# Attention and quantized FFN on one core: stacks loaded a batch earlier, FFN weights loaded and summed later

## What is computed

```python
# x: (8, 128, 256) float32, cond: (8, 256) mask; 16 heads of 8 channels
Q, K, V = proj(Wq), proj(Wk), proj(Wv)                    # per batch, from x
att = einsum('bhqd,bhkd->bhqk', Q, K) / sqrt(8) + b
att = att * m + (1 - m) * -1e30;  att = softmax(att)
y = einsum('bhqk,bhkd->bhqd', att, V)
# FFN over the channels; activations quantized per token to 8 bits,
# weights to -1, 0, 1 times the mean of their absolute values
h = silu(bit_linear(y, w_gate)) * bit_linear(y, w_up)
out = x + bit_linear(rms_norm(h) * ln_weight, w_down)     # (8, 128, 256)
```

## Time and profile before

| | |
|---|---|
| median of 3 runs | 175.95 us (175.43 to 178.37) |
| the profiled execution | 175.54 us, its span 173.7 us |
| busy in the span | PE 145.5, DVE 143.1, ACT 125.2, POOL 96.2 us |
| mean granted TensorE clock | 0.979 |

### The profile page before, as it was taken

The page is one execution under the profiler, slowest core; times in us unless marked ns, Lnnn a source line. Parts: engine busy times, 40 slices in busy tenths (PEclk is TensorE's granted clock), DMA queues, the critical chain, the costliest instruction groups (busy, mean ns, idle before and its releaser), DMA issues.

```text
span 173.7 us, 4104 instructions
## 1 busy us (share of the span) xinstructions
PE 145.5 (84%) x1395; PEld 68.1 (39%) x1402; DVE 143.1 (82%) x209; ACT 125.2 (72%) x253; POOL 96.2 (55%) x175
## 2 busy tenths in 40 slices
PE   7979894999989979969979999977699586887672
PEld 3664552433433423323323333322223264454561
DVE  6789895599999979869879898953678999999981
ACT  2041489699879869849869889878698928886651
POOL 5989507705808929829729629522040884677520
PEclk9999999699999999999999999999999969999999
DMA  4895988632232322622232320000000000010002
GB/s 118 287 167 131 303 304 284 167 91 55 61 93 57 74 75 57 203 65 57 68 80 59 92 52 3 3 6 5 0 0 4 0 2 0 30 34 30 32 30 91
DMA packets 20124, 14.19 MB, mean 82 GB/s; under 512 B 2160, under 2 KB 19080, under 8 KB 20104
## 3 DMA queue, kind: packets, MB, share of 16 engines
q1 hardware_dynamic: 17624, 10.91, 22.5%
q10 hardware_dynamic: 2480, 3.02, 6.2%
HBM read 6.17 MB, written 1.07 MB: 42 GB/s over the span
## 4 chain that ended last, share of the span: by engine, by line
PE 26%; SPq 17%; ACT 13%; DVE 12%; DMA 11%; issue 11%; ACTq 5%; POOL 2%; DVEq 0%; POOLq 0%
SPq L264 15%; PE y_ps L1000 7%; DMA k_st<-parts 6%; PE s_ps L962 5%; DMA w_f<-in_wuT 5%; ACT probs L523 4%; ACTq L264 4%; PE t_ps L980 4%; DVE hid L813 2%; DVE hw L822 2%; SPq L325 2%; ACT h_T L644 2%; PE y_ps L1041 1%; ACT hid_sq L627 1%; PE t_ps L1120 1%
## 5 line engine op out<-in xcount | busy, mean ns | idle before, releaser
L879 DVE TENSOR_REDUCE maxes<-s_ps 128x4 f32<-128x1024 f32 x64 | 76.1, 1217 | 11.4 <-PE s_ps L962 11.2
L523 ACT ACTIVATE probs<-t_ps 128x512 f32<-128x512 f32 x128 | 71.3, 593 | 15.9 <-PE t_ps L980 14.2
L962 PE MATMUL s_ps<-k_st,q_st 64*128 64x256 bf16 x256 | 44.9, 277 | 4.8 <-DMA k_st<-parts 4.5
L980 PE MATMUL t_ps<-q_st,k_st 64*128 64x256 bf16 x256 | 43.8, 277 | 4.7 <-ACT probs L523 3.1
L1000 PE MATMUL y_ps<-probs,v_pad 128*18 128x256 f32 x512 | 39.1, 388 | 0.0
L962 PEld LDWEIGHTS s_ps<-k_st,q_st 64*128 64x128 bf16 x256 | 15.8, 94 | 34.1 <-issue 12.8
L409 POOL TENSOR_SCALAR nm_parts<-maxes 128x16 bf16<-128x16 f32 x16 | 3.3, 208 | 33.6 <-DVE maxes L879 27.2
L478 POOL TENSOR_TENSOR hw<-hid,ln_bc 128x512 f32<-128x512 f32 x8 | 10.2, 1273 | 19.7 <-DVE hid L802 14.9
L1081 PE MATMUL s_ps<-w_q,ffn_x 128*128 128x512 bf16 x59 | 16.9, 387 | 3.3 <-DVE hid L813 1.5
L980 PEld LDWEIGHTS t_ps<-q_st,k_st 64*128 64x128 bf16 x256 | 14.7, 94 | 11.3 <-ACT probs L523 6.0
L1000 PEld LDWEIGHTS y_ps<-probs,v_pad 128*18 128x18 f32 x512 | 9.7, 96 | 13.6 <-issue 12.1
(11 more groups left out here) (106 smaller groups left out, 238.4 us busy)
## 6 DMA issues: line engine op xcount, KB each, us to landing
q_st<-parts SPq DMA_DIRECT2D x48, 64.0 KB
k_st<-parts SPq DMA_DIRECT2D x36, 64.0 KB
w_f<-in_wgT ACTq DMA_DIRECT2D x2, 512.0 KB, 5.4
w_f<-in_wuT ACTq DMA_DIRECT2D x2, 512.0 KB, 8.3
w_f<-in_wdT SPq DMA_DIRECT2D x2, 512.0 KB, 4.7
out<-o_sb SPq DMA_DIRECT2D x8, 128.0 KB, 1.7
k_st<-parts ACTq DMA_DIRECT2D x12, 64.0 KB
x_sb<-in_x SPq DMA_DIRECT2D x2, 256.0 KB, 4.0
```

The lines of the kernel that those rows point to most:

```text
L523: act.activation(probs[:, t % NP_RING].rearrange("p e t -> p (e t)"), src, ACT.Exp, scale=SCALE)\
L879: dve.tensor_reduce(dst[:, :, s, :], s_ps[:, c % 2], AX.X, ALU.max).then_inc(s_maxed, 1)
L962: mm = pe.matmul(s_ps[:, c % 2, i, e, :], q_st[b % RING][rows, hp, qt * P:qt * P + P], k_st[b % RING][rows, hp, :], start=True, stop=True)
L980: mm = pe.matmul(t_ps[:, u % T_BANKS, e, :], k_st[b % RING][rows, hp, kt * P:kt * P + P], q_st[b % RING][rows, hp, :], start=True, stop=True)
```

## The change

Four things change; what is computed, and how, does not.

1. SP loads the stack of batch n+3 in step n, where it loaded that of batch n+2. The order within a step is new: second maxima of batch n; rows, bias and all six high parts of batch n+3; first maxima of batch n+1; six low parts of batch n+3. Batch 1's stack is loaded ahead of the loop.
2. ACT issues weight pieces 0 to 3 in slot (-1, 7), a step's length later; SP issues 4 and 5 (and the last part of the mask) at the end of step 0 instead of step -1.
3. The sums are moved and dealt out anew: ACT takes q = 0, 2, 4, 5 in slots (0, 4), (0, 7), (1, 4), (2, 3); DVE takes q = 1, 3 in (0, 5), (1, 0). `sum_last_weights` becomes `sum_weights` on DVE, the same instruction with the piece as its argument.
4. The total moves from slot (1, 1) to (3, 1), the means on DVE from (1, 2) to (3, 2), and POOL's passes from steps 2 to 6 into steps 3 to 6: four of the nine now stand in step 5, where three did.

```diff
-WEIGHT_SUM_SLOTS = {(-1, 4): (0,), (-1, 5): (1,), (-1, 7): (2,), (0, 0): (3,), (0, 5): (4,)}
-LAST_SUM_SLOT = (0, 6)
-WEIGHT_TOTAL_SLOT = (1, 1)
+WEIGHT_SUM_SLOTS = {(0, 4): 0, (0, 7): 2, (1, 4): 4, (2, 3): 5}
+VECTOR_SUM_SLOTS = {(0, 5): 1, (1, 0): 3}
+WEIGHT_TOTAL_SLOT = (3, 1)
...
             load_bias(0)
+            load_rows(1)
+            load_bias(1)
+            load_high(sp, 1, 0)
+            load_low(sp, 1, (0,))
+            load_mask(sp, 2)
             for n in range(FIRST, LAST + 1):
-                if has(n + 2):
-                    load_rows(n + 2)
-                    load_bias(n + 2)
-                    load_high(sp, n + 2, 0)
                 if has(n):
                     load_max_rows(n, 1)
...
-                if n == -1:
-                    load_low(sp, 1, (0,))
-                    load_mask(sp, 2)
-                elif has(n + 2):
-                    load_high(sp, n + 2, 1)
-                    load_low(sp, n + 2, (0, 1))
+                if has(n + 3):
+                    load_rows(n + 3)
+                    load_bias(n + 3)
+                    load_high(sp, n + 3, 0)
+                    load_high(sp, n + 3, 1)
                 if has(n + 1):
                     load_max_rows(n + 1, 0)
-                if n == -1:
+                if has(n + 3):
+                    load_low(sp, n + 3, (0, 1))
+                if n == 0:
                     load_weights(sp, 4)
                     load_weights(sp, 5)
                     load_mask(sp, 3)
...
-            for q in range(4):
-                load_weights(act, q)
...
-                    for q in WEIGHT_SUM_SLOTS.get((n, k), ()):
-                        sum_weights(q)
+                    if (n, k) == (-1, 7):
+                        for q in range(4):
+                            load_weights(act, q)
+                    if (n, k) in WEIGHT_SUM_SLOTS:
+                        sum_weights(WEIGHT_SUM_SLOTS[n, k])
...
-                    if (n, k) == LAST_SUM_SLOT:
-                        sum_last_weights()
-                    if (n, k) == (1, 2):
+                    if (n, k) in VECTOR_SUM_SLOTS:
+                        sum_weights(VECTOR_SUM_SLOTS[n, k])
+                    if (n, k) == (3, 2):
                         mean_weights()
...
-            weight_steps = {2: ((), (0,)), 3: ((), (1,)), 4: ((), (2,)), 5: ((3, 4), (5,)), 6: ((6, 7), (8,))}
+            weight_steps = {3: ((), (0,)), 4: ((), (1,)), 5: ((2, 3), (4, 5)), 6: ((6, 7), (8,))}
```

More of the change, by code:

```diff
@@ L199, in adaln_ffn_kernel @@
         abs_done = sem("abs_done")
-        last_abs_done = sem("last_abs_done")
+        vector_abs_done = sem("vector_abs_done")
         wscale_step = sem("wscale_step")
@@ L443, in quantize_weights @@
                     pool.wait_ge(wscale_step, 3)
-                    pool.wait_ge(abs_done, min(2 * m + 2, 5))
-                    if m == 2:
-                        pool.wait_ge(last_abs_done, 1)
+                    pool.wait_ge(abs_done, len(WEIGHT_SUM_SLOTS))
+                    pool.wait_ge(vector_abs_done, len(VECTOR_SUM_SLOTS))
                     pool.tensor_scalar(w_f[:, m, :], w_f[:, m, :], w_inv[:, m:m + 1], MAGIC, ALU.mult, ALU.add)\
@@ L574, in sum_weights @@
                 act.wait_ge(w_in[q], 16)
-                if q:
-                    act.wait_ge(abs_done, q)
+                act.wait_ge(abs_done, sorted(WEIGHT_SUM_SLOTS.values()).index(q))
                 act.activation(hid_sq[:, :], w_f[:, m, 1024 * part:1024 * part + 1024], ACT.Abs,
@@ L732, in _, with sum_weights @@
                 clear_stacks(r)
-            def sum_last_weights():
-                dve.wait_ge(w_in[5], 16)
-                dve.tensor_reduce(w_abs[:, 5:6], w_f[:, 2, 1024:2048], AX.X, ALU.add, apply_absolute_value=True)\
-                   .then_inc(last_abs_done, 1)
+            def sum_weights(q):
+                m, half = divmod(q, 2)
+                dve.wait_ge(w_in[q], 16)
+                dve.tensor_reduce(w_abs[:, q:q + 1], w_f[:, m, 1024 * half:1024 * half + 1024], AX.X, ALU.add,
+                                  apply_absolute_value=True).then_inc(vector_abs_done, 1)
             def mean_weights():
@@ L927, in add_weight_sums @@
                 pe.wait_ge(small_const, 4)
-                pe.wait_ge(abs_done, 5)
-                pe.wait_ge(last_abs_done, 1)
+                pe.wait_ge(abs_done, len(WEIGHT_SUM_SLOTS))
+                pe.wait_ge(vector_abs_done, len(VECTOR_SUM_SLOTS))
                 pe.matmul(dst[:, 0:6], ones_f[:, :], w_abs[:, :], start=True, stop=True).then_inc(unit_ready, 1)
```

## The result

The changed kernel takes 178.83 us (median of 4 runs, 177.17 to 179.62) where the kernel before takes 175.69 beside it (4 runs): 1.018 times as long, 95% interval 1.012 to 1.024. It is slower, by 3.1 us, where 4.4 us of gain were forecast. The profiled execution took 179.62 us, the longest of the four; its span is 177.8 and its mean granted clock 0.971.

The account below looks back on a forecast made before the run. PE, nearly full, needs about 11.84 us a step; the rest is waits for late stacks, plus a slow start. Terms: -3.4 - 1.0 - 1.7 + 0.9 + 0.8 = -4.4, giving 171.1 profiled, 171.5 us median; range 169.2 to 174.6.

Parts of the forecast that it names:

- The failed step: SP's new order, judged in step 2: first maxima go out at 61.9, an us earlier than 62.95, so no loss.
- The slower rival: Weights issued from 25.1 make batch 0's second maxima 5.9 us late in slot (0, 5): +3.2, 179.2 us; chance 0.05.
- The slow clock: Step 0: PE's idle piece shrinks from 1.63 to some 0.6 us, so the 3.4 us half-speed stretch doesn't come: -1.7 us.
- Weights off the start: Start of step 0: four issues and sums leave ACT's way, exponentials start near 27.6 instead of 28.6: -1.0 us.
- Stacks: Starts of steps 1 to 4 (batches 3 to 6): the wait for late `k_st` parts goes: -3.4 us, bounds 0 to 4.2.
- Sums: Steps 0 to 2: three more places where ACT sums among exponentials hold PE up by 0.30 each: +0.9 us.
- Piece 4: Slot (1, 4): issued at 40.7, landed at 45.1, ACT there at 44.2 and waiting 0.9: +0.8 us.
- T1: Time of batch 2's first maxima: 40.3 in the kernel before, forecast at 37.9.
- SP as the bound: Rival: issues lengthen by a tenth, steps take 12.1 us, first maxima late at the starts: -1.3, 174.6 us; chance 0.12.

Follow-up runs that it names:

- spread03: `w45_later` with weight pieces 0 to 3 issued one at a time by ACT behind the first exponentials of step 0, sums moved to follow; 173.56 us, ratio 0.990.
- max_sooner: Changed kernel with pieces 0, 1 at the start, 2 to 5 by ACT in step 0, batch 0's first maxima ahead of three `k_st` parts; 175.64 us.
- stacks_only: The kernel before with only the stacks loaded a batch earlier by SP, in the changed kernel's order of issues; 174.48 us, ratio 0.990.
- w03_early: The changed kernel with weight pieces 0 to 3 issued by ACT where the kernel before issues them; 179.08 us, ratio 1.017.
- both_moved: The changed kernel with the edits of `w03_early` and `w45_later` together; 177.47 us, ratio 1.009.
- sp_between: `max_sooner` with pieces 2 to 5 taken from ACT into SP's own order, at fixed distances from the maxima; 174.35 us, ratio 0.993.
- w45_later: The changed kernel with pieces 4, 5 and the last mask part behind batch 1's second maxima, sums in (2, 3) and (2, 7); 177.34 us, ratio 1.010.

## Why the prediction was wrong

*The failed step* is the price of the maxima's landing in a stretch full of weights, which the sum put at nothing ("I see no loss there"). The prediction took 2.0 us, from the earlier trace rows, "amid the same traffic", as evidence against its slower rival. That row is the kernel before at a DMA share of 0.39, with its four pieces issued six to eight us earlier. In the changed kernel the share is 0.91 over the same transfer, since the pieces start with it: 4.80 us, and 5.21 behind pieces 4 and 5. The number was right and its condition wasn't carried along; the traffic was not the same.

*The slower rival* named this mechanism, priced it within 0.4 us of the time that came (179.2 against 178.83), gave it 0.05, and had the place wrong. That its time came so close is luck: it has one wait of 5.9 us where there were two, of 4.76 and 3.42, and the other terms of its sum were off as well. It looked only at the second maxima of batch 0 in (0, 5); those went out at 32.37 and nobody waited. Of the first maxima the prediction asked when they are issued, 25.0 (25.05 measured), and took "the transposed scores are there at about 27.0" from that; they came at 29.9. The second maxima of batch 1, directly behind pieces 4 and 5 in the new order of SP's queue, were not examined at all, though the order shows them there. The prediction cited the Trainium skill ("DMA: Bandwidth & Descriptors", Issuing engines are not separate DMA queues) for transfers of both queues interleaving on the same engines, and set a row against it. By these runs the Trainium skill is right for small transfers too: the pieces were on ACT's queue, the maxima on SP's, and they took 1.94, 3.51 and 4.85 us with none, one and four of them.

*The slow clock*, -1.7, came with the other sign. PE was idle for longer, not shorter, and the stretches at 0.50 are 5.9 us and most of 3.5 us instead of 3.4; half of what was added, about 3 us, is lost. The prediction tied this term to the wait, which was right, so it fell with the wait. No trace is free of such a stretch in these steps: where the first wait was short, 1.32 us in `spread03`, the clock was still 0.58 over 29 to 33; in `max_sooner` (0.87) it held through that stretch and fell later, behind another wait. The size of the term is doubtful too. Of the 90 executions of the kernel before that stand beside the experiments, 8 had a mean clock of 1.00 and took 175.2 us in the median, 23 had 0.99 and took 175.8; a stretch of 3.4 us at half speed is 0.01 of that mean. So the same kernel has the stretch in one execution and not in another, which the prediction said no run showed, and it seems to cost nearer 0.6 us than 1.7. The tails say the same: the kernel before has a stretch at 0.50 in its tail (140 to 142), the changed kernel has none, and the tails last equally long.

*Weights off the start*, -1.0: step -1 gained it, 9.52 instead of 10.51 us, and the exponentials came at 30.54 instead of 27.6.

*Stacks*, -3.4: right in kind and near in size. PE no longer waits for `k_st<-parts`, the steps that were to be 11.8 to 12.2 are 11.89, 11.83 and 12.33, steps 2 to 5 gain 2.8 us together, and `stacks_only` measures -1.6 us net of a start that was worse. The condition "the maxima must not be late" was tested on step 2 only ("I see no loss there"); in the start, where batch 2's stack is new ahead of the first maxima, it fails once the pieces are in flight as well (`w03_early`, `both_moved`).

*Sums*, +0.9: at most nothing in the slots of the change (0.994 alone, the interval touching 1); two on ACT in one step do cost, 13.33 us in `spread03` against 11.50 without them. *Piece 4*, +0.8: 0.27; it left at 45.58 and not at 40.7, but T1 was 43.5 and not 37.9. *SP as the bound* was rejected for the middle, rightly (11.5 a step), and is what seems to hold the start of `sp_between`.

The sum by measured terms of the two traces: step -1 -1.0, steps 0 and 1 +4.1 and +3.6, the rest -2.8, the very start +0.1: +4.0, and the spans say +4.1 (177.8 against 173.7). The medians say +3.1; the profiled execution was the longest of its four.

## What to carry to other kernels

Before a bulk load is moved, list the small transfers that someone waits for at once and see which of them fall within a few us of it, on whatever queue: they pay for it, and the engine that waits may pay again in its clock. A landing time read off a row holds for the DMA share of that row. Where a load has slack, spread it over places where no such transfer is near, and check that the issuing queue still reaches the urgent ones in time.

## What the runs showed of the hardware

- A 12 KB transfer between places in SBUF landed in 1.9 to 2.3 us up to a DMA share of 0.5 (one of 2.92 among them), in 2.5 to 3.5 us between 0.5 and 0.8, and in 3.3 to 6.5 us above 0.8, whichever queue the bulk was on (the table above). The same program gave 4.85 us in one execution (the changed kernel) and 6.54 in another (`w45_later`, the same up to there).
- An issue of a part, 0.60 us as a rule, took up to 1.9 us beside a 16 KB packet of the instruction queue (56 of 1,190, every one within 0.6 us of such a packet). Weight pieces in flight did not lengthen it by themselves: 1.99 us for three parts in `both_moved`.
- A wait of 4.76 us was followed by a 5.9 us stretch at the 1.2 GHz level, one of 3.42 us by most of 3.5 us at it, and one of 1.32 us by a drop some 2.5 us after PE had resumed (0.58 over 29:33 in `spread03`). But PE waited 1.60 us at 77.62 in the kernel before and 1.90 us at 33.70 in `max_sooner` and kept its full clock. Of the waits between 1.3 and 2.0 us, some are followed by a slow stretch and some are not.
